# Cross attention and a spline FFN over four batches: a rolled loop with one batch in advance, against an unrolled program that works on three batches at once

## The chip, the cores and the metric

One core of a Trainium2 chip runs the whole kernel. The metric is the device time of one execution in microseconds (us). The kernel before takes 311.19 us (median of 3 runs, 310.43 to 312.0). TensorE (PE) multiplies matrices, VectorE (DVE), ScalarE (ACT) and GpSimd (POOL) work elementwise, and SyncE (SP) starts the DMAs. Each runs its own list of instructions in order; semaphores tie the lists together.

## The reference

For each of 4 batches (512 tokens, width 512) the kernel computes

```
query = ctx @ Wq.T + bq ;  key = ctx @ Wk.T + bk             # ctx 512x256, width 128
att   = softmax(query @ key.T)                               # 512x512
x     = x + einsum('ln,mn->lm', layernorm(x), att)           # no scale, over tokens
gate  = layernorm(x) @ gate_w.T ; up = layernorm(x) @ up_w.T # 2048 wide
x     = x + (silu(gate) * up) @ down_w.T
```

The three FFN weights are Catmull-Rom splines of some 8,000 control points each. The kernel never builds them whole: a weight is a few smooth functions plus a short "residual", so that a projection is a small product with the functions (`project`, `replicate`) and the gate and up products have only 128 rows.

## The kernel before, in words

All sums run in fp32; where a factor is rounded to the 1-pass format (fp32r), a high and a low part are kept, so that many steps are a pair: ACT copies the rounded part out of PSUM, DVE subtracts it from the exact value (`split_prob`, `project`, `half_split`, `down_split`).

- **One list for all engines.** A program calls stages in an order written out by hand (`attention_only`, then `ffn`); every engine has a class with the same stage names and issues only its own part. So the call order is each engine's instruction order.
- **Prologue** (`attention_only`, L429 on): builds the weight tables (`spread`/`residual` 0 to 23, `node_weights`, `jump_inputs`/`jumps`, `down_nodes`), and runs the attention of batch 0. `keep_warm` calls put 60 products of ones on PE between the stages.
- **Pass** (`ffn`, L536 on): the FFN of batch b, and in its gaps the attention of a = b+1. It runs as a hardware loop for b = 0 to 2, then once more for b = 3 without attention.
- In a pass: `project`, `qk` (query and key), four `replicate` (two products, an ACT copy and two DVE operations each, which put the 4 functions of a class into the tile `mv`), 16 gates (`gate_up` on PE, SiLU on ACT, product on DVE: `activate`, L1018; rounding into `ih` on POOL: `round_inter`, L1188), between them `energy`, `softmax`, `prob_t`, `split_prob`; then `down` (64 products with `ih`), `xm` (48 products: attention times x), `add_xm` (adds to x, statistics, `normalise`), `norm_t`/`cast_t` (transposes of the normalised x), `down_tail` (adds the result to `xres` and stores it).
- `prob` is scaled by 1/sum on DVE (`scale`), the low part of x comes from POOL (`low_x`, L1120), and POOL copies x to `xres` in `project` (L1175) once the stores of the batch before are done. POOL also computes the two small reciprocal roots of the layernorms (`ve`, then `rstd`: L1076/L1078 and L1159/L1161).

## Time and profile before

| what | us |
|---|---|
| median of the runs | 311.19 |
| the profiled execution's own time | 310.87 |
| its span, first to last instruction | 308.7 |
| PE busy (82%) | 254.3 |
| DVE busy (65%) | 202.2 |
| POOL busy (50%) | 154.3 |
| ACT busy (45%) | 138.5 |

The span is what the instructions cover; 2.2 us of the execution's time lie around it. Busy time of PE counts pipelined products whose ends are modelled, so it overstates the work. The chain of work that ended last gives PE 36%, POOL 22%, DVE 10%, and 25% to "issue", where the profile shows nothing that was waited for. The granted TensorE clock is 0.912 on average.

### The profile page before, as it was taken

What the parts mean: (1) busy time and instruction counts of PE and PEld (TensorE: products, weight loads), DVE (VectorE), ACT (ScalarE), POOL (GpSimd) and SP (SyncE); (2) the same over time, 40 slices, a digit from 0 to 9 for tenths busy, and PEclk for the clock granted to TensorE, in tenths of its full rate; (3) what the DMA queues carried; (4) which work ended last, traced back from release to release, by engine and by line L of the source; (5) the groups of instructions that cost most, each with busy time, mean ns of one, the idle gap of its engine ahead of it and who ended that gap; (6) DMA issues with size and microseconds to landing.
All of it is one profiled execution on the core that took longest, in us unless ns stands there. A gap on an engine that the chain in (4) does not pass through costs nothing.

```text
span 308.7 us, 4074 instructions
## 1 busy us (share of the span) xinstructions
PE 254.3 (82%) x1320; PEld 158.4 (51%) x1320; DVE 202.2 (65%) x348; ACT 138.5 (45%) x229; POOL 154.3 (50%) x158
## 2 busy tenths in 40 slices
PE   5979519868797889998867999979679999576995
PEld 1323107632333646786334568863436689253484
DVE  1665795674759886575598765756988557478523
ACT  3043414310736586225758642267589131745420
POOL 0987930263675559321463692304829722077810
PEclk9775857995969799999999899999999999959999
DMA  6799600000007000001280000013500000300003
GB/s 221 289 271 381 264 0 0 1 1 2 0 13 328 0 3 0 2 0 68 74 333 0 0 0 0 0 70 95 243 0 0 0 0 14 122 0 2 0 2 136
DMA packets 6938, 22.65 MB, mean 73 GB/s; under 512 B 1168, under 2 KB 2320, under 8 KB 5456
## 3 DMA queue, kind: packets, MB, share of 16 engines
q1 hardware_dynamic: 6928, 22.52, 20.1%
q8 instruction: 6, 0.10, 0.1%
q14 instruction: 4, 0.03, 0.0%
HBM read 18.32 MB, written 4.19 MB: 73 GB/s over the span
## 4 chain that ended last, share of the span: by engine, by line
PE 36%; issue 25%; POOL 22%; DVE 10%; ACT 4%; DMA 1%; SPq 1%; POOLq 0%; DVEq 0%; ACTq 0%
POOL ih L1188 10%; PE bank L1348 5%; POOL xl L1120 4%; PE bank L1350 4%; PE bank L1349 4%; PE bank L1440 4%; POOL xres L1175 3%; PE bank L1222 3%; PE bank L1400 3%; PE bank L1235 2%; POOL gw L1102 2%; PE bank L1325 2%; PE bank L1248 2%; PE bank L1447 1%; PE bank L1414 1%
## 5 line engine op out<-in xcount | busy, mean ns | idle before, releaser
L1188 POOL TENSOR_TENSOR ih<-inter,ones 128x512 fp32r<-128x512 f32 x64 | 64.5, 1040 | 38.4 <-DVE inter L1018 38.4
L1400 PE MATMUL bank<-mv,gw 128*128 128x512 f32 x128 | 47.5, 469 | 17.8 <-DVE inter L1018 9.2
L1018 DVE TENSOR_TENSOR inter<-inter,bank 128x512 f32<-128x512 f32 x64 | 42.1, 682 | 6.6 <-ACT inter L828 5.1
L828 ACT ACTIVATE inter<-bank 128x512 f32<-128x512 f32 x64 | 37.0, 597 | 20.1 <-PE bank L1400 18.6
L1400 PEld LDWEIGHTS bank<-mv,gw 128*128 128x128 f32 x128 | 23.7, 202 | 40.8 <-DVE inter L1018 18.0
L1440 PEld LDWEIGHTS bank<-d_r,ih 128*128 128x128 f32 x256 | 35.3, 188 | 7.9 <-issue 5.0
L1440 PE MATMUL bank<-d_r,ih 128*128 128x288 f32 x256 | 38.2, 299 | 0.0
L799 ACT ACTIVATE qk<-bank,nmr,rstd 128x512 f32<-128x512 f32 x16 | 12.5, 780 | 43.2 <-PE bank L1350 26.9
L1159 POOL TENSOR_TENSOR ve<-mv,eps 128x1 f32<-128x1 f32 x16 | 5.6, 347 | 47.5 <-DVE mv L989 47.5
L1175 POOL TENSOR_TENSOR xres<-x,ones 128x2048 f32<-128x2048 f32 x4 | 14.4, 3600 | 28.8 <-DMA out<-xres 28.5
L1348 PE MATMUL bank<-ph,xh 128*128 128x512 f32 x64 | 25.5, 399 | 2.1 <-POOL xl L1120 2.1
L1010 DVE SCALAR_TENSOR_TENSOR mv<-zd,masks,bank 64x512 fp32r<-64x512 f32 x32 | 23.9, 747 | 4.8 <-ACT zd L821 3.9
L1350 PE MATMUL bank<-ph,xl 128*128 128x512 f32 x64 | 25.0, 391 | 0.0
L1349 PE MATMUL bank<-pl,xh 128*128 128x512 f32 x64 | 24.9, 390 | 0.0
L804 ACT ACTIVATE prob<-bank 128x512 f32<-128x512 f32 x16 | 9.6, 597 | 28.8 <-PE bank L1363 28.6
L1222 PE MATMUL bank<-warm 128*128 128x512 bf16 x60 | 21.0, 515 | 1.5 <-DVE warm L863 1.5
L1235 PE MATMUL bank<-ctxT,wqk 128*128 128x512 f32 x32 | 20.3, 767 | 0.0
L984 DVE TENSOR_TENSOR x<-x,qk 128x512 f32<-128x512 f32 x16 | 11.3, 706 | 12.4 <-ACT qk L799 12.4
L1290 PE MATMUL bank<-knots,spread 64*128 64x288 bf16 x32 | 7.1, 331 | 14.5 <-DVE knots L974 8.7
L1414 PE MATMUL bank<-inter,d_u 64*32 64x512 f32 x256 | 17.6, 635 | 1.2 <-DVE mv L1010 1.2
L1120 POOL TENSOR_TENSOR xl<-xT,xh 128x2048 fp32r<-128x2048 f32 x4 | 18.3, 4570 | 0.0
L1107 POOL TENSOR_TENSOR d_r<-prod 128x288 fp32r<-128x288 f32 x16 | 13.3, 851 | 8.0 <-DVE prod L926 7.7
(98 smaller groups left out, 434.0 us busy)
## 6 DMA issues: line engine op xcount, KB each, us to landing
x<-in_x SPq DMA_DIRECT2D x4, 1024.0 KB, 4.9
xT<-in_xT SPq DMA_DIRECT2D x4, 1024.0 KB, 7.2
out<-xres SPq DMA_DIRECT2D x16, 256.0 KB, 2.0
rd<-in_d_r SPq DMA_DIRECT2D x1, 2304.0 KB, 22.4
ctxT<-in_ctxT SPq DMA_DIRECT2D x4, 512.0 KB, 7.1
d_coef<-in_d_coef SPq DMA_DIRECT2D x1, 1024.0 KB, 15.8
d_pt<-in_d_node SPq DMA_DIRECT2D x1, 1024.0 KB, 17.4
knots<-in_d_knot SPq DMA_DIRECT2D x1, 640.0 KB, 13.2
```

Source lines behind the costliest of these rows:

```text
L828: nc.scalar.activation(inter[:, m], gbank[m % 2][:], ACT.Silu).then_inc(s["silu_done"], 1)
L1010: V.scalar_tensor_tensor(mv[part, 2 * t + n], zs[part, t % 2].bitcast(f32), z_low[part], zbank[t % 2][part], ALU.mult, ALU.add).then_inc(s ...
L1018: V.tensor_tensor(inter[:, m], inter[:, m], ubank[m % 2][:], ALU.mult).then_inc(s["mult_done"], 1)
L1120: G.tensor_tensor(xl[:], xT[:], xh[:].bitcast(f32), ALU.subtract).then_inc(s["xsplit_done"], 1)
L1188: G.tensor_tensor(ih[:, m], inter[:, m], ones[:, 0].broadcast_to([P, TOK]), ALU.mult).then_inc(s["ih_done"], 1)
L1222: mm(zdbank[:], warm[:, 0:P], warm[:], start=True, stop=True)
L1235: last = mm(abank[n][:], wqk[:, n, c], ctxT[:, c], start=c == 0, stop=c == CTX // P - 1)
L1348: mm(abank[t % 2][:], xh[:, n, c], ph[:, n], start=n == 0, stop=False)
L1349: mm(abank[t % 2][:], xh[:, n, c], pl[:, n], start=False, stop=False)
L1350: last = mm(abank[t % 2][:], xl[:, n, c], ph[:, n], start=False, stop=n == NT - 1)
L1400: mm(dst[m % 2][:], gw[:, n, m // 2, m % 2 * P:(m % 2 + 1) * P], mv[:, m // 2], start=True, stop=True).then_inc(s[done], 1)
L1440: mm(in_blocks(obank[t], m % PHASES), ih[:, m, t * P:(t + 1) * P], d_r[:, m], start=m == 0, stop=False, skip_group_check=True)
```

## The change

The loop is unrolled in Python, and the program becomes `attention_first`, then for every b the stages `gates(b)` and `downs(b)`, with a = b+1 and c = b+2:

- `attention_first` runs the attention of batch 0, `project(0)`, and `qk`, `energy`, `softmax` of batch 1. The fillers shrink from 60 to 6; `down_nodes` now stands after the first half of `xm(0)`, and half of the 16 small sums in `residual` moves from POOL to DVE (`upper`).
- `gates(b)` holds the 16 gates of b and, between them, `prob_t`, `xm` and `add_xm` of a. `downs(b)` holds the products of `down` for b, `norm_t`, `cast_t`, `project` and `functions` of a, and `qk`, `energy`, `softmax` of c.
- `replicate` goes. `functions` forms the functions for four classes at a time (4 products, 2 ACT copies, 2 DVE subtractions a batch), and 24 DMAs a batch, of 20 rows of 2 KB, copy them from `zs` to their rows in `mv` (`place` on SP). A gate waits for 12 of them.
- `prob` of batches 1 to 3 is scaled on POOL. x has three buffers, the result is added into x in place, and the `xres` copy goes. `inter` shrinks from 16 to 8 tiles.
- Rounding: POOL rounds every activation of the first three passes; in the last, ACT rounds every fourth.

```diff
-        def attention_only(st):
+        def attention_first(st):
...
+            for n in range(NT):
+                st.xm(0, n, 0)
+            st.jumps()
+            for r in range(8, 10):
+                st.spread(r)
+                st.residual(r)
+            st.turn()
+            st.down_nodes()
+            for t in range(2):
+                st.scale_xm(0, t)
...
+            for t in range(NT):
+                st.energy(1, t)
+                st.softmax(1, t)
+            st.scale(1)
+            st.stats(1)
+            st.mean_shift(1)
+            st.silu_table(0)
...
+        def downs(st, b):
+            a, c = b + 1, b + 2
+            if c < B:
+                st.qk(c, 0)
+            if a < B:
+                st.normalise(a, 3)
+            st.down_basis(b, 3)
+            if c < B:
+                st.qk(c, 1)
+            st.half_split(b)
+            if c < B:
+                st.exp_table()
+            st.down(b, 0)
...
+            if c < B:
+                for t in range(2, NT):
+                    st.energy(c, t)
+                    st.softmax(c, t)
+                st.scale(c)
+                for h in range(2):
+                    st.split_x(c, h)
+            st.down_tail(b, 2)
+            st.add_out(b, 2)
+            st.down(b, 3)
+            if c < B:
+                st.stats(c)
+                st.mean_shift(c)
+                st.silu_table(c)
+            st.down_tail(b, 3)
+            st.add_out(b, 3)
...
+            def place(b, j):
+                sp.wait_ge(s["zs_done"], 2 * b + j + 1)
+                for i in range(CLS):
+                    a = CLS * j + i
+                    base = 0 if a % 2 else HALF
+                    for k, z in enumerate((0, 1, 0)):
+                        rows_to = slice(base + k * G_FN, base + (k + 1) * G_FN)
+                        sp.dma_start(mv[rows_to, a].bitcast(f32), zs[QUAD * i:QUAD * i + G_FN, 2 * j + z].bitcast(f32)).then_inc(s[("z0_in", "z1_in")[j]], 16)
...
                 def scale(b):
-                    pass
+                    if b:
+                        pool.wait_ge(s["rinv_done"], b + 1)
+                        for t in range(NT):
+                            G.tensor_tensor(prob[:, t], prob[:, t], rinv[:, t].broadcast_to([P, TOK]), ALU.mult).then_inc(s["prob_done"], 1)
...
                     for n, (dst, read, done) in enumerate(((gbank, "silu_done", "g_mm"), (ubank, "mult_done", "u_mm"))):
                         if m >= 2:
                             pe.wait_ge(s[read], MT * b + m - 1)
-                        if n == 1 and a is not None:
-                            pe.wait_ge(s["exp_done"], NT * (a + 1))
+                        elif b:
+                            pe.wait_ge(s["out_added"], NT * (b - 1) + 2 * n + m + 1)
```

How the lists of the engines differ is seen at three places. First POOL, in a loop pass of the kernel before, from the last roundings on: `xl` is the low part of x of the next batch, and `ve` and `rstd` (128x4) its layernorm's root.

```order
L1188 TENSOR_TENSOR ih<-inter,ones 128x512 [waits mult_done]
L1119 REGISTER_ALU
L1120 TENSOR_TENSOR xl<-xT,xh 128x2048 [waits xh_done]
L1076 TENSOR_TENSOR ve<-mv,eps 128x4 [waits mv1_done,consts_set]
L1078 TENSOR_TENSOR rstd<-ve,neghalf 128x4 [waits ve1_done]
```

The same place in the changed kernel, after the roundings of pass 0 and up to those of pass 1:

```order
L1270 TENSOR_TENSOR ih<-inter,ones 128x512 [waits mult_done] x2
L1242 TENSOR_TENSOR ve<-mv,eps 128x1 [waits mv2_done]
L1244 TENSOR_TENSOR rstd<-ve,neghalf 128x1 [waits ve2_done]
L1175 TENSOR_TENSOR prob<-prob,rinv 128x512 [waits rinv_done]
L1175 TENSOR_TENSOR prob<-prob,rinv 128x512 x3
L1202 TENSOR_TENSOR xl<-xT,xh 128x1024 [waits xh_done] x2
L1152 TENSOR_TENSOR ve<-mv,eps 128x4 [waits xm_scaled,mv1_done,consts_set]
L1154 TENSOR_TENSOR rstd<-ve,neghalf 128x4 [waits ve1_done]
L1270 TENSOR_TENSOR ih<-inter,ones 128x512 [waits mult_done] x9
```

Four scalings of `prob`, which wait for the sums of all exponentials, now stand ahead of `xl` and of the root, and all of them ahead of the next pass's roundings.

Second DVE at the end of a pass of the kernel before: the results of the batch are added, the last casts done, and the next pass begins with `zp` (`project`).

```order
L1045 TENSOR_TENSOR xres<-xres,bank 128x512 [waits x1_kept,out_mm] x2
L997 CAST mv<-prob 64x512 [waits xn2t_first] x3
L1045 TENSOR_TENSOR xres<-xres,bank 128x512 [waits x1_kept,out_mm] x2
L997 CAST mv<-prob 64x512 [waits xn2t_first]
L638 REGISTER_ALU
L638 COMPARE_AND_BRANCH
L1004 TENSOR_TENSOR zp<-bank,zp 128x512 [waits zp_hi]
```

In the changed kernel, from the first results of pass 0 (`x<-x,bank`) to the first gate products of pass 1 (`inter`):

```order
L1123 TENSOR_TENSOR x<-x,bank 128x512 [waits out_mm] x2
L970 TENSOR_REDUCE nmax<-bank 128x1 [waits energy_mm] x2
L1086 TENSOR_TENSOR zs<-bank,zs 128x512 [waits zs_hi] x2
L970 TENSOR_REDUCE nmax<-bank 128x1 [waits energy_mm] x2
L974 RECIPROCAL rinv<-rsum 128x4 [waits exp_done]
L1123 TENSOR_TENSOR x<-x,bank 128x512 [waits out_mm]
L947 BN_STATS bst<-x 128x6 [waits x2_in]
L947 BN_STATS bst<-x 128x6 x3
L952 BN_AGGR mv<-bst 128x2 [waits stats1,consts_set]
L952 BN_AGGR mv<-bst 128x2 x3
L957 SCALAR_TENSOR_TENSOR nmr<-mv,rstd 128x4 [waits rstd1_done]
L1123 TENSOR_TENSOR x<-x,bank 128x512 [waits out_mm]
```

`nmr`, which waits for POOL's root, now stands ahead of the last addition of the batch; in the kernel before it stood after `half_split` and ahead of the first `add_xm`.

Third SP in a pass of the kernel before, from the load of the next x to the first store:

```order
L684 ISA [waits x1_kept,xn2_done]
L684 DMA x<-in_x 128x2048
L686 DMA xT<-in_xT 128x2048 [waits xn2T_mm]
L688 ISA
L689 ISA [waits qk_mm]
L689 DMA ctxT<-in_ctxT 128x1024
```

and in pass 0 of the changed kernel:

```order
L672 DMA x<-in_x 128x2048 [waits dv_done,res_done]
L708 DMA ctxT<-in_ctxT 128x1024 [waits qk_mm]
L704 DMA xT<-in_xT 128x2048 [waits xsplit_done]
L722 DMA out<-x 128x512 [waits out_added] x2
L718 DMA mv<-zs 20x512 [waits zs_done]
L718 DMA mv<-zs 20x512 x11
L718 DMA mv<-zs 20x512 [waits zs_done]
L718 DMA mv<-zs 20x512 x11
```

The 24 copies of `place` stand behind two stores and ahead of the other two.

## Rows read from the trace of the kernel before

**Rows 1.** Busy time by stretch, us from the span's start.

```profile
core 0: us, PE busy (x) PEld busy (x) DVE busy (x) ACT busy (x) POOL busy (x), PEclk, DMA share, GB/s
0.00:46.00 46.00, 30.03 (x115) 10.28 (x115) 28.00 (x45) 12.87 (x21) 30.41 (x33) 0.74 0.70 239
46.00:93.50 47.50, 40.69 (x159) 22.18 (x159) 29.84 (x48) 15.62 (x25) 20.49 (x25) 0.82 0.03 8
...
118.00:154.00 36.00, 33.12 (x189) 23.75 (x189) 20.91 (x42) 15.51 (x23) 14.48 (x14) 1.00 0.08 30
154.00:178.80 24.80, 20.01 (x107) 11.89 (x106) 20.90 (x36) 17.88 (x33) 14.69 (x15) 0.93 0.27 106
...
273.00:291.70 18.70, 15.90 (x76) 9.23 (x77) 14.95 (x22) 10.29 (x18) 13.65 (x15) 0.85 0.00 1
291.70:308.70 17.00, 13.83 (x106) 10.78 (x105) 4.74 (x7) 1.68 (x3) 2.62 (x3) 1.00 0.17 63
```

**Rows 2.** Timeline of DVE: start, duration; the last gate products of two passes.

```profile
177.49 1.28 DVE L1018 TENSOR_TENSOR inter<-inter,bank 128x512 f32<-128x512 f32 x2
...
287.52 4.17 DVE L1018 TENSOR_TENSOR inter<-inter,bank 128x512 f32<-128x512 f32 x6 [1.90 <-ACT inter L828]
```

**Rows 3.** Costliest groups by line: busy us, mean ns, idle before and its releaser.

```profile
L1188 POOL TENSOR_TENSOR ih<-inter,ones 128x512 fp32r<-128x512 f32 x64 | 64.5, 1040 | 38.4 <-DVE inter L1018 38.4
L1018 DVE TENSOR_TENSOR inter<-inter,bank 128x512 f32<-128x512 f32 x64 | 42.1, 682 | 6.6 <-ACT inter L828 5.1
L1120 POOL TENSOR_TENSOR xl<-xT,xh 128x2048 fp32r<-128x2048 f32 x4 | 18.3, 4570 | 0.0
...
L1078 POOL TENSOR_TENSOR rstd<-ve,neghalf 128x4 f32<-128x4 f32 x4 | 4.1, 1018 | 0.3
```

**Rows 4.** Timeline of PE: query products at both clocks, `xm` products one after another.

```profile
55.19 0.39 PE L1349 MATMUL bank<-pl,xh 128*128 128x512 f32 x1
55.42 0.39 PE L1350 MATMUL bank<-ph,xl 128*128 128x512 f32 x1
...
86.54 3.78 PE L1235 MATMUL bank<-ctxT,wqk 128*128 128x512 f32 x4
...
148.40 1.98 PE L1235 MATMUL bank<-ctxT,wqk 128*128 128x512 f32 x4
```

**Rows 5.** Timeline of ACT: a table load, an exponential, two casts.

```profile
103.81 1.28 ACT L735 ACT_TABLE_LOAD   x1
...
106.67 0.68 ACT L735 ACTIVATE prob<-bank,nmax 128x512 f32<-128x512 f32 x1
...
143.04 0.59 ACT L805 ACTIVATE mv<-bank 64x512 fp32r<-64x512 f32 x1
143.66 0.60 ACT L804 ACTIVATE prob<-bank 128x512 f32<-128x512 f32 x1
```

**Rows 6.** Timeline of POOL and DVE where both read tiles in SBUF.

```profile
35.87 5.36 POOL L1135 TENSOR_TENSOR d_coef<-d_coef,d_pt 128x512 f32<-128x512 f32 x4
36.05 4.06 DVE L966 SCALAR_TENSOR_TENSOR win<-win 64x512 f32<-64x512 f32 x1
...
41.87 0.68 DVE L971 SCALAR_TENSOR_TENSOR win<-knots 64x512 f32<-64x512 f32 x1
...
61.58 2.01 POOL L1107 TENSOR_TENSOR d_r<-prod 128x288 fp32r<-128x288 f32 x2
62.08 0.84 DVE L984 TENSOR_TENSOR x<-x,qk 128x512 f32<-128x512 f32 x1
```

**Rows 7.** Timeline of SP's issues: start, duration.

```profile
8.83 1.75 SPq L647 DMA_DIRECT2D knots<-in_d_knot  x1
...
153.30 0.36 SPq L684 DMA_DIRECT2D x<-in_x  x1
153.75 0.38 SPq L686 DMA_DIRECT2D xT<-in_xT  x1
```

**Rows 8.** DMA issues: KB each, median us from issue to landing.

```profile
out<-xres SPq DMA_DIRECT2D x16, 256.0 KB, 2.0
```

More of the change, by code:

```diff
@@ L528, in attention_only @@
+            st.project(0)
+            for n in range(2):
+                st.qk(1, n)
+            for j in range(2):
+                st.functions(0, j)
+            for h in range(2):
+                st.split_x(1, h)
             for r in range(20, 24):
                 st.spread(r)
[L531 to L540 removed]
+                st.residual(r)
@@ new lines, in gates @@
+            gate(7)
+            if more:
+                st.xm(a, 3, 0)
+                for t in range(2):
+                    st.scale_xm(a, t)
+            gate(8)
+            if more:
+                st.add_xm(a, 0)
+                st.xm(a, 0, 1)
+            gate(9)
+            if more:
+                st.normalise(a, 0)
+                st.add_xm(a, 1)
+                st.xm(a, 1, 1)
+            gate(10)
+            st.down_basis(b, 1)
+            gate(11)
+            if more:
+                st.normalise(a, 1)
+                st.xm(a, 2, 1)
@@ L693, in _ @@
-            sp.wait_ge(s["qk_mm"], 2)
-            sp.dma_start(ctxT[:], d["ctxT"][1]).then_inc(s["ctx_in"], 16)
-            with sp.Fori(0, B - 2) as b:
-                batch(b, True)
-            batch(B - 2, False)
-            for t in range(NT):
-                store(B - 1, t)
-            sp.wait_ge(s["out_stored"], 16 * NT * B + 1)
+                sp.dma_start(out[b, t], x[b][:, t]).then_inc(s["out_stored"], 16)
+            columns(1)
+            sp.wait_ge(s["consts_set"], 1)
+            for j in range(2):
+                place(0, j)
@@ L702, in _ @@
+            for b in range(B):
+                if b + 2 < B:
+                    rows(b + 2)
+                    context(b + 2)
+                    columns(b + 2)
+                for t in range(2):
+                    store(b, t)
+                if b + 1 < B:
+                    for j in range(2):
+                        place(b + 1, j)
+                for t in range(2, NT):
+                    store(b, t)
+            sp.wait_ge(s["out_stored"], 16 * NT * B)
         @block.scalar
```

855 lines of the change are left out of this document (436 added, 419 removed).

## The prediction

> **What bounds the kernel now.** I read the stretches first, then DVE's timeline to cut them at the right points, then the groups by line. The cuts are the ends of a pass's sixteenth gate product on DVE: 118.0 for pass 0 (a border of [rows 1]), 178.8 for pass 1 (177.49 + 1.28) and 291.7 for pass 3 (287.52 + 4.17) [rows 2]. So the kernel is a prologue with the gates of batch 0 (118.0 us), passes of 60.8 us, and 17.0 us from the last product to the end. In the pass from 118.0 to 178.8 PE is busy 33.1 + 20.0 = 53.1 of 60.8 us, DVE 41.8, ACT 33.4, POOL 29.2 [rows 1]. No engine fills it; PE is nearest, at a granted clock of 1.00 and 0.93, nearly the upper level (2.4 GHz). In the prologue the clock is 0.74 and 0.82, a mixture of both levels. POOL waits for DVE's products before its roundings (38.4 us in all), not DVE for POOL [rows 3]. What the deeper pipeline can win is therefore the difference between 60.8 and some 53 a pass, and the prologue's and the last pass's waits. Whether it does hangs on the waits that its order brings, so I followed the changed lists from one cut to the next.
>
> **Between two passes (from product 16 of b to the low part of `prob` of c).** Where PE needs a semaphore only from work that is done, it goes on at 0.23 us for a product of 512 columns (55.19 to 55.42) [rows 4].
> - PE does a quarter of `down_basis` (1.0) and the key half of `qk` (1.8 at the upper level: four parts recorded as 1.98) [rows 4]; ACT then adds the bias (0.7), copies two halves (1.2), loads the exponential's table (1.3 and a small operation, 1.5) and casts 4 x 2 x 0.62 = 5.0 [rows 5]; one more copy (0.6) and one subtraction (0.7) give `zd`: 12.9 us after the cut.
> - Then DVE runs in order: PE's tail and `zp` (1.5), two additions, two maxima, two subtractions of `functions`, two maxima, each pair 1.3 (0.68 for one, 0.60 from one to the next) [rows 2, 3], with ACT's two exponentials (0.68 each [rows 5]) and two copies in between (2), and the last exponential (0.9): 22.0 us.
> - POOL now has `prob`: four operations of the form of `ih`, 4.1 us, then `xl` 4.6, then the root 1.3 [rows 3]: 10 us after the reciprocal. `nmr` on DVE waits for this root. Behind it on DVE stand the last addition of b, which frees the PSUM bank of the second gate's up product, the low parts of `prob`, and every gate product of the next pass; PE can do two transposes and three gate products and then stands. This cover did not exist before: POOL's `xl` and root stood where DVE had `half_split` and statistics. Here DVE has 3.5 us of other work for the 10.
> - Sum: 22.0 + 0.2 + 10.0 + 0.8 = 33 us. It is at least 26 if the POOL chain were hidden, at most 36 if the casts and PE's clock come out worse.
>
> The 24 copies by DMA are hidden. SP gets `zs` at about 19.5 us. Two issues of the loop are 0.45 us apart (153.30 to 153.75) [rows 7], a store lands after 2.0 us [rows 8], so the first twelve are down at 19.5 + 5.4 + 2.0 = 27 us and the other twelve at 32 us, needed only at the ninth gate. If the cover at 33 us goes, the first twelve cost up to 5 us less than they take now, so nothing below 27. No row shows a copy inside SBUF: the lower bound is nothing, the upper 1.75 us an issue, the longest in the trace [rows 7], by which they would be down at 42 us. I take 0.45, since the queue is not full there as it was then.
>
> **Gates.** PE has 32 gate products and 48 of `xm`, 80 x 0.23 = 18.2 us, transposes and partial products of some 5: 23.6. DVE has 16 products and 4 low parts, at 0.60 from one to the next 12, and three of the four additions to x with their statistics and normalisations, some 2.2 each: 18.5. They don't lie side by side. DVE works behind PE until the first half of `xm` is done, some 16 us in; after that the additions and normalisations hold back gate products (in order on DVE), and the rest is DVE's own 11 to 12 us with a wait for a root here and there. So 16.5 + 12 + 1 for a port that it shares with POOL (below) = 29.5. The lower bound is 24.8, what the gates with four maxima, four low parts and their exponentials take now [rows 1]; the upper 33. What `replicate` gave back (six DVE operations net, 4 us a pass, and an ACT copy or two) is in this sum. POOL's 16 roundings take 16.6 us [rows 3] and are no bound; the four that ACT takes over in the last pass save nothing there. The `xres` copy ended before POOL had a product to round [rows 3], so its going counts as nothing.
>
> So a pass takes 33 + 29.5 = 62.5 us, against 60.8.
>
> **Prologue, up to the low parts of `prob` of batch 1.** Milestones: 14 us, both `qk` products of batch 0, now ahead of all tables and at the lower clock level (3.78 us for four parts [rows 4] instead of 1.98); 34, the tables, softmax and node weights, a chain of DVE operations; 43, the root, four jump inputs on POOL, low parts of `prob`; 49, the first half of `xm`; then a new wait. POOL does two sums and the four multiplications of `down_nodes` (5.4 us [rows 6]), DVE and ACT, in order, wait for them and do 3.9 more, and only then may ACT scale `xm` and free the banks: 60.5, with PE idle for 11 us and back at the lower level. 68, the second half of `xm`; 78, additions, roots and residuals in turn; 84, casts; 94, `project`, `qk`, `functions`; 108, softmax of batch 1, held by the last residuals, whose POOL half stands behind `xl`; 112 to 113, `prob` on POOL and the root. I take 112; the bounds are 100 (the upper clock level throughout, and half of the new wait gone) and 120. The gates of batch 0 end at 112 + 29.5 = 141.5 us, 23.5 later than now, but with `xm` of batch 1 done.
>
> **The end.** Pass 3 has no attention. After product 16 of pass 2 the chain to `zs` is short by the exponentials and the query (14 us), the first twelve copies take 5.4 + 2.0: 21.5. The gates of batch 3: 0.7 each for 16, 1.4 for the first to pass through, 1 for the lower clock after PE's wait of 3 us: 13.5. Then 17.0 as now [rows 1].
>
> **Sum.** 112 + 29.5 + 2 x 62.5 + 21.5 + 13.5 + 17.0 = 318.5 us of span, against 308.7. With the 2.2 us around the span of the profiled execution (310.87) it is 320.7; that execution stands 0.3 below the median of 311.19, which leaves the forecast at 320.
>
> **What speaks against the change beside this.** In the trace a DVE operation on two tiles in SBUF that began 0.18 us after POOL's four multiplications took 4.06 us, where the next of its kind took 0.68; an addition to x under two POOL sums took 0.84 [rows 6]; gate products, with one input in PSUM, keep 682 ns beside the roundings [rows 3]. The Trainium skill's page "SBUF — State Buffer", section "Who interferes with whom", says that a DVE instruction with two SBUF inputs, or a `tensor_scalar` in a 2-port mode, and a GpSimd instruction that reads SBUF exclude each other for the whole instruction. The trace agrees in the first case and hardly in the second (0.16 us).
>
> **Rivals.**
> - A: the pipeline does what its depth allows. For it speaks that no engine has over 53.1 us in a pass [rows 1]; against it the root behind `xl`. If the POOL chain is covered, 27 + 27 us a pass: 112 + 27 + 2 x 54 + 52 = 299, so 301 us.
> - B (slower still): additions and normalisations now run while POOL rounds without pause. If each of the seven of a pass waits for half to a whole rounding of 1.04 us, or now and then loses to several as at 36.05 [rows 3, 6], it is 3 to 4 us more a pass in three passes, less the 1 counted: 328 us. It decides as soon as DVE, not PE, sets the second half of the gates.
> - C: the prologue keeps pace, at 102 instead of 112: 310 us, no change.
> - D: the small copies are slow, 1.75 us an issue [rows 7]: 42 instead of 33 us twice, and 14 us later in the last pass: 353 us. The skill's page "DMA: Bandwidth & Descriptors", section "Rules for kernel authors", says that transfers under 64 KB pay mostly overhead and are to be merged; these have 40 KB. No row here shows one.
>
> **How the numbers follow.** The forecast has 0.48 (its own range 313 to 327), A 0.20, B 0.20, C 0.09, D 0.03. From the low bound of A to above B, 301 to 335 us, leaves out some 2 in 10. A measurement of this kernel can tell 0.5% from no change, 309.6 to 312.7 us. Faster: A, and a third of C: 0.23. Same: the rest of C and the forecast's edge: 0.08. Slower: 0.69.
>
> **What would show it.** Right: `nmr` in passes 1 and 2 waits some 6 us for POOL's root and PE stands meanwhile after the third gate product; products 16 lie 61 to 64 us apart; ACT's first scaling of `xm` in the prologue follows POOL's `d_coef`; the first gate stands near 112. Wrong: gates that follow each other without this wait, passes of 54 us, or a first gate before 100.

## The result and the profile after

The changed kernel takes 330.75 us (median of 4, 329.06 to 331.17) against 310.81 of the kernel before on the same chip: 1.064 times as long, 95% interval 1.058 to 1.069. The sign and the range held; the size did not: 19.9 us were lost where the forecast had 8.8. The profiled execution took 329.06 us, its span 327.3 us; it was the fastest of the four (the others' spans are 328.6 to 329.4 us), so what follows takes apart some 1.7 us less than the median lost.

The span of after in stretches. The cuts are the forecast's own: the first low part of `prob` (115.1), the end of the sixteenth gate product of a pass on DVE (143.5, 204.2, 265.3, 310.5), the low parts again (176.0, 236.7, two rows left out), the first gate of the last pass (292.7; PE started it at 292.56). Columns as in [rows 1].

```profile
0.00:46.00 46.00, 26.61 (x108) 12.84 (x109) 32.95 (x62) 14.23 (x25) 20.32 (x22) 0.70 0.80 282
46.00:115.10 69.10, 38.76 (x132) 22.29 (x131) 36.33 (x62) 19.66 (x34) 32.00 (x36) 0.70 0.07 15
115.10:143.50 28.40, 26.36 (x141) 17.50 (x140) 20.60 (x33) 14.32 (x24) 18.49 (x21) 0.95 0.25 91
143.50:176.00 32.50, 25.91 (x151) 19.59 (x151) 16.97 (x36) 18.69 (x33) 11.99 (x11) 0.89 0.14 38
176.00:204.20 28.20, 26.03 (x137) 17.11 (x137) 20.40 (x34) 12.64 (x21) 18.45 (x21) 0.94 0.34 123
...
265.30:292.70 27.40, 20.81 (x125) 16.14 (x126) 10.12 (x18) 8.14 (x14) 2.16 (x3) 0.87 0.13 39
292.70:310.50 17.80, 15.54 (x80) 7.12 (x80) 10.72 (x16) 10.58 (x19) 12.18 (x12) 0.83 0.19 56
310.50:327.30 16.80, 13.54 (x96) 11.63 (x96) 4.74 (x8) 2.31 (x4) 0.04 (x1) 0.96 0.16 63
```

Set beside the forecast, term by term (us of span; the last column sums to the 8.8 that are missing between 318.5 and 327.3):

| term | forecast | measured | difference |
|---|---|---|---|
| prologue to the low parts of batch 1 | 112 | 115.1 | +3.1 |
| gates of batch 0 | 29.5 | 28.4 | -1.1 |
| between passes, gates (pass 1) | 33 + 29.5 | 32.45 + 28.25 | -1.8 |
| between passes, gates (pass 2) | 33 + 29.5 | 32.45 + 28.6 | -1.45 |
| last pass: to its first gate | 21.5 | 27.3 | +5.8 |
| last pass: its 16 gates | 13.5 | 17.95 | +4.45 |
| the end | 17.0 | 16.8 | -0.2 |

So 13.35 us were missing in three terms, and 4.55 us that the others had too much hid a third of it: the total is nearer to the forecast than its terms are.

Pass 1 is as long as before, 60.7 us against 60.8, and pass 2 is 1.8 us longer; PE has 25.9 + 26.0 busy us in pass 1, one less than the 53.1 of [rows 1]. What the change gives in the last pass (53.7 before, 45.2 now) does not pay for a prologue that is 25.5 us longer (118.0 to 143.5). The unrolling does not show as a cost of its own: "issue", where nothing that the profile shows was waited for, has 5% of the chain that ended last, against 25% before. The groups by line and the waits (columns of the waits: us in total, times, longest), to be read against [rows 3]:

```profile
L1270 POOL TENSOR_TENSOR ih<-inter,ones 128x512 fp32r<-128x512 f32 x60 | 65.6, 1108 | 55.5 <-DVE inter L1094 55.2
...
L1094 DVE TENSOR_TENSOR inter<-inter,bank 128x512 f32<-128x512 f32 x64 | 42.7, 681 | 27.4 <-ACT inter L881 26.7
...
DVE nmr L957 <- POOL rstd L1154: 17.2, 4, 6.6
...
PE bank L1442 <- ACT qk L849: 10.4, 1, 10.4
...
PE bank L1510 <- DMA mv<-zs: 9.2, 4, 5.9
```

Three waits stand there that the kernel before did not have at this size: DVE for POOL's root, PE in the middle of `xm` of the prologue, and PE for the small copies. The first was there before, but short:

```profile
DVE nmr L895 <- POOL rstd L1078: 4.4, 3, 1.5
```

The first two were forecast, each within 0.6 us. The third was forecast to be hidden.

The timeline between pass 0 and pass 1, POOL, then DVE, then PE:

```profile
165.36 4.03 POOL L1175 TENSOR_TENSOR prob<-prob,rinv 128x512 f32<-128x512 f32 x4 [19.38 <-DVE rinv L974]
169.35 4.67 POOL L1202 TENSOR_TENSOR xl<-xT,xh 128x1024 fp32r<-128x1024 f32 x2
173.98 0.20 POOL L1152 TENSOR_TENSOR ve<-mv,eps 128x4 f32<-128x4 f32 x1
174.25 1.01 POOL L1154 TENSOR_TENSOR rstd<-ve,neghalf 128x4 f32<-128x4 f32 x1
...
175.30 0.16 DVE L957 SCALAR_TENSOR_TENSOR nmr<-mv,rstd 128x4 f32<-128x4 f32 x1 [6.59 <-POOL rstd L1154]
...
172.58 1.62 PE L1510 MATMUL bank<-mv,gw 128*128 128x512 f32 x3 [1.17 <-DMA mv<-zs]
176.12 0.80 PE L1510 MATMUL bank<-mv,gw 128*128 128x512 f32 x1 [1.91 <-DVE x L1123]
```

This is the forecast's chain: four scalings, `xl`, the root, then `nmr` after 6.59 us, and PE stops after the third gate product, since the addition that frees the fourth's bank stands behind `nmr` on DVE. PE's first product there already waited 1.17 us for the copies; the wait for the root came behind that and ended last.

The last pass: SP's 24 issues, with those of the prologue ahead for comparison; PE's first 16 partial products and 16 products of `down`, with 16 later ones of `down`; then PE's first gates and its ninth.

```profile
95.48 18.16 SPq L718 DMA_DIRECT2D mv<-zs  x24
...
281.94 17.97 SPq L718 DMA_DIRECT2D mv<-zs  x24
...
265.33 1.96 PE L1530 MATMUL bank<-inter,d_u 64*32 64x512 f32 x16 [3.34 <-DVE inter L1094]
267.23 4.21 PE L1560 MATMUL bank<-d_r,ih 128*128 128x288 f32 x16
...
280.86 2.28 PE L1560 MATMUL bank<-d_r,ih 128*128 128x288 f32 x16
...
292.56 6.39 PE L1510 MATMUL bank<-mv,gw 128*128 128x512 f32 x14 [5.91 <-DMA mv<-zs]
...
301.35 1.69 PE L1510 MATMUL bank<-mv,gw 128*128 128x512 f32 x5 [0.71 <-DMA mv<-zs]
```

The issues stand 0.75 us apart (17.97 / 24; 0.76 in the prologue, where SP's issue before them ended 57 us earlier), not the 0.45 that the forecast took from two loads [rows 7], so the first twelve are down 10.6 us after the first issue instead of 7.4. That is 3.2 of the 5.8 us. The other 2.6 are a chain to `zs` of 16.7 us (265.3 to 281.9) where the forecast had 14, and the trace shows where they arose. After 3.34 us of waiting PE is granted 0.50, the lower level (1.2 GHz), from 265.3 to 271.3: the 16 partial products take 1.96 us instead of the 1.09 of the other passes, and 16 products of `down` 4.21 instead of 2.28. That is 2.8 us, and the transposes of the normalised x stand behind them. In the prologue run below, which changes nothing in the last pass, the same 16 products of `down` took 2.88 us, and the chain 15.3.

### The profile page after: what moved, and what is told of

It reads as the page before. It is cut to its first block, busy times and chain, and to the rows that moved or that the text cites. A ratio compares the mean times of both kernels' runs of the same rounds, so it can differ in the third digit from the quotient of the medians.

```text
span 327.3 us, 3646 instructions
## 1 busy us (share of the span) xinstructions
PE 243.9 (75%) x1250; PEld 160.2 (49%) x1250; DVE 190.3 (58%) x328; ACT 131.2 (40%) x226; POOL 146.1 (45%) x158
## 4 chain that ended last, share of the span: by engine, by line
PE 45%; DVE 21%; POOL 11%; ACT 10%; SPq 6%; issue 5%; DMA 2%; DVEq 0%; ACTq 0%; POOLq 0%
PE bank L1560 7%; PE bank L1510 6%; SPq L718 5%; PE bank L1320 4%; POOL xl L1202 4%; PE bank L1442 4%; PE bank L1443 3%; PE bank L1444 3%; PE bank L1530 3%; DVE inter L1094 3%; DVE bst L947 3%; PE bank L1398 2%; PE bank L1566 2%; DVE bst L1060 2%; PE bank L1346 2%
## 5 line engine op out<-in xcount | busy, mean ns | idle before, releaser
L881 ACT ACTIVATE inter<-bank 128x512 f32<-128x512 f32 x64 | 37.2, 596 | 45.3 <-PE bank L1510 44.9
L1442 PE MATMUL bank<-ph,xh 128*128 128x512 f32 x64 | 27.5, 430 | 10.4 <-ACT qk L849 10.4
L1175 POOL TENSOR_TENSOR prob<-prob,rinv 128x512 f32<-128x512 f32 x12 | 12.1, 1041 | 44.1 <-DVE rinv L974 44.1
L1398 PE MATMUL bank<-masks,prob 128*128 128x128 f32 x64 | 14.5, 391 | 19.1 <-POOL prob L1175 10.7
L1202 POOL TENSOR_TENSOR xl<-xT,xh 128x1024 fp32r<-128x1024 f32 x8 | 18.7, 2357 | 13.5 <-ACT xh L809 13.5
L1398 PEld LDWEIGHTS bank<-masks,prob 128*128 128x128 f32 x64 | 11.4, 203 | 23.3 <-POOL prob L1175 12.3
L781 ACT ACTIVATE prob<-bank,nmax 128x512 f32<-128x512 f32 x16 | 10.9, 686 | 25.6 <-DVE nmax L970 25.6
L801 ACT ACTIVATE ph<-bank 128x512 fp32r<-128x512 f32 x16 | 9.6, 598 | 28.4 <-PE bank L1398 28.4
L1320 PE MATMUL bank<-ctxT,wqk 128*128 128x512 f32 x32 | 18.1, 705 | 3.6 <-DMA wqk<-in_wkT 3.6
L1442 PEld LDWEIGHTS bank<-ph,xh 128*128 128x128 f32 x64 | 13.4, 209 | 14.3 <-ACT qk L849 10.7
L997 DVE TENSOR_TENSOR prod<-bank,rd 128x576 f32<-128x576 f32 x16 | 11.7, 750 | 11.6 <-PE bank L1384 7.1
L1466 PE MATMUL bank<-masks,xn 128*128 128x128 f32 x64 | 11.4, 316 | 8.9 <-DVE xn L1071 6.0
```

What stands on the lines that cost most here:

```text
L881: nc.scalar.activation(inter[:, m % DEPTH], gbank[m % 2], ACT.Silu).then_inc(s["silu_done"], 1)
L1202: G.tensor_tensor(xl[:, part], xT[:, part], xh[:, part].bitcast(f32), ALU.subtract).then_inc(s["xsplit_done"], 1)
L1320: last = mm(abank[n], wqk[:, n, c], ctxT[:, c], start=c == 0, stop=c == CTX // P - 1)
L1398: last = nc.tensor.transpose(pbank[t % 2][:, m * P:(m + 1) * P], prob[:, m, t * P:(t + 1) * P], ident)
L1442: mm(abank[t % 2], xh[:, n, c], ph[:, n], start=n == 0, stop=False)
```

## The experiments

All kernels are the changed one with the edit shown. The edits are shortened: `...` stands for lines left out, and within lines types, semaphores and helper code are left out too. The gates of batch 0 ended between 143.4 and 145.7 us in the profiled runs of after and of seven kernels that change nothing ahead of them on the engines, and the medians come from several chips, on which the kernel before took 309.4 to 311.7 us; so the runs are compared by their stretches: gates of batch 0 done, then from one sixteenth product to the next, then to the end.

| kernel | median us | span | gates of 0 done | pass 1 | pass 2 | last pass | end |
|---|---|---|---|---|---|---|---|
| before | 310.81 | 308.7 | 118.0 | 60.8 | 59.3 | 53.7 | 17.0 |
| after | 330.75 | 327.3 | 143.5 | 60.7 | 61.05 | 45.2 | 16.8 |
| early root | 322.92 | 320.7 | 143.4 | 57.8 | 57.9 | 44.8 | 16.7 |
| two queues | 328.40 | 326.9 | 144.7 | 60.7 | 61.0 | 43.7 | 16.7 |
| early taps | 327.16 | 324.8 | 140.6 | 60.9 | 61.2 | 45.3 | 16.8 |
| 16 copies | 324.93 | 323.2 | 143.5 | 60.7 | 61.05 | 41.2 | 16.7 |
| no ACT rounding | 330.46 | 329.4 | 145.7 | 60.7 | 61.1 | 45.2 | 16.8 |
| gates ahead | 327.50 | 325.5 | 145.05 | 60.7 | 61.1 | 42.0 | 16.7 |
| prologue | 317.05 | 315.7 | 132.8 | 61.1 | 61.2 | 43.8 | 16.8 |
| first four together | 303.56 | 302.6 | 134.2 | 55.55 | 54.85 | 41.3 | 16.8 |
| scale on DVE | 334.59 | 332.7 | 146.4 | 62.3 | 61.9 | 45.3 | 16.8 |
| copies hidden | 324.00 | 323.1 | 145.7 | 60.7 | 61.0 | 38.9 | 16.8 |
| four banks | 325.10 | 323.7 | 145.0 | 60.7 | 61.0 | 40.2 | 16.8 |
| all, scale on DVE | 304.70 | 301.9 | 131.8 | 58.5 | 58.3 | 36.5 | 16.8 |
| all, scale on POOL | 296.99 | 293.3 | 131.3 | 54.8 | 54.9 | 35.6 | 16.7 |
| all, `xl` behind | 297.83 | 295.4 | 134.6 | 54.0 | 54.4 | 35.6 | 16.8 |

**Early root.**

```diff
             st.half_split(b)
             if c < B:
+                st.stats(c)
                 st.exp_table()
...
             st.down_split(b)
+            if c < B:
+                st.mean_shift(c)
             st.down(b, 1)
...
             if c < B:
-                st.stats(c)
-                st.mean_shift(c)
                 st.silu_table(c)
```

> The layernorm statistics of batch c and their root on GpSimd are moved ahead of the scaling of prob and of xl (to the casts of the same pass, where GpSimd has nothing to do for 19 us); nothing else changes. Theory (the forecast's step between two passes): nmr no longer waits 6.6 us for the root, so the low parts of prob start when ACT has copied the first half, near 171.2 instead of 175.98, and the third addition no longer holds PE; the first gate stays where it is, since it waits for the copies (172.6). Passes 1 and 2 get some 3 us shorter each (57.5 and 58 instead of 60.7 and 61.05 between the sixteenth products), 6.5 us in all: span 321, time 324. Rival: the gates behind it are bound by PE (26.4 of 28.4 us busy), or xm waits for xl instead, and most of it is given back: under 2 us in all, 329.

Measured: 2.9 and 3.1 us off the two passes, 6.6 of span. DVE and PE at the same place:

```profile
155.81 0.15 DVE L958 SCALAR_TENSOR_TENSOR nmr<-mv,rstd 128x4 f32<-128x4 f32 x1
...
171.13 0.69 DVE L1008 TENSOR_TENSOR pl<-bank,ph 128x512 fp32r<-128x512 f32 x1 [3.47 <-ACT ph L802]
...
172.48 2.04 PE L1511 MATMUL bank<-mv,gw 128*128 128x512 f32 x4 [1.16 <-DMA mv<-zs]
```

`nmr` waits for nothing, the low parts start at 171.13 instead of 175.98, and PE's first gate has not moved, since it waits for the copies. The step stands as forecast: the root's place alone cost 3 us a pass. The low parts came 4.85 us earlier; the other 2 were kept by the copies, as the four edits together show below.

**Two queues for the copies of the last pass.**

```diff
-                for i in range(CLS):
+                copies(sp, b, j, range(2 if b in SHARED else CLS))    # SHARED = (3,)
...
+                    if t == 2 and b + 1 in SHARED:                    # act, down_tail
+                        for j in range(2):
+                            act.wait_ge(s["zs_done"], 2 * (b + 1) + j + 1)
+                            copies(act, b + 1, j, range(2, CLS))
```

> Of the 24 copies of the last pass 12 (classes 2 and 3 of each four) are issued by ScalarE, which is idle there, and 12 by SyncE; passes before are unchanged. Theory (the copies are late because one queue issues them 0.75 us apart): six issues and the landing take 4.5 + 1.6 us, so the first gate of the last pass starts near 288 instead of 292.6, the ninth gate waits for nothing, and the sixteenth product comes 6 us earlier: span 321, time 324.5. Rival (the DMA engines or SBUF take that long for 20 rows of 2 KB, or both queues share one issuer): the copies land as late as before, and nothing changes within 1.5 us.

```profile
283.19 10.05 ACTq L661 DMA_DIRECT2D mv<-zs  x12
293.37 1.09 ACT L886 ACTIVATE inter<-bank 128x512 f32<-128x512 f32 x2 [10.45 <-issue]
...
290.47 2.05 PE L1518 MATMUL bank<-mv,gw 128*128 128x512 f32 x4 [2.61 <-DMA mv<-zs]
```

The copies did land earlier: PE's first product came 7.3 us after the first issue instead of 10.6. But ScalarE issued all its twelve, for both halves, in 10.05 us before the first SiLU, which starts at 293.37, the same time as in after (this pass began 1.2 us later). Of the 6 us 1.5 were seen (45.2 to 43.7). The edit exchanged one wait for another; it shows that the queue's issues were late, not what hiding them is worth.

**Early taps.** POOL's four multiplications get a stage of their own behind `jump_inputs`; `down_nodes` (sums on DVE, copy on ACT) moves behind the residuals 12 and 13.

```diff
             st.jump_inputs()
+            st.down_taps()            # POOL: the four multiplications
...
-            st.down_nodes()
             for t in range(2):
                 st.scale_xm(0, t)
...
+            st.down_nodes()
```

> In the prologue the four multiplications on GpSimd stand right behind the jump inputs (where GpSimd was idle for 6.8 us), and the sums on VectorE and the copy on ScalarE behind the second half of xm; nothing else changes. Theory (the wait of 10.4 us of PE in the middle of xm sets the prologue): ScalarE scales the first half near 51 instead of 60.6, and everything up to the first gate comes 9 to 10 us earlier: first low part of prob near 106, span 318, time 321. Rival (another chain sets the prologue: the 16 residuals on VectorE and GpSimd, or the multiplications now hold VectorE's jump operations as long as before): under 3 us.

ScalarE scaled at 53.16 instead of 60.63, yet the first low part came at 111.8 instead of 115.1. Of the 7.5 us 3.8 went to the sums and their wait for ScalarE, which now stand between two additions to x, and 1 to query products at the lower clock level. And not all of the expected 9 to 10 arose in the first place, because POOL now runs beside DVE's jump operation:

```profile
45.49 4.11 DVE L1039 SCALAR_TENSOR_TENSOR win<-win 64x512 f32<-64x512 f32 x1
...
45.28 5.47 POOL L1220 TENSOR_TENSOR d_coef<-d_coef,xn 128x512 f32<-128x512 f32 x4
```

That is the pair of [rows 6] once more: 4.11 us for an operation that takes 0.68 alone. The rival's bound, under 3 us, is nearer than the theory's; with the run-to-run difference of the prologue the size is not settled by this run.

**16 copies instead of 24.**

```diff
-                    for k, z in enumerate((0, 1, 0)):
-                        rows_to = slice(base + k * G_FN, base + (k + 1) * G_FN)
-                        sp.dma_start(mv[rows_to, a], zs[QUAD * i:QUAD * i + G_FN, 2 * j + z])
+                    part = slice(QUAD * i, QUAD * i + G_FN)
+                    sp.dma_start(mv[base:base + 2 * G_FN, a], zs[part, 2 * j:2 * j + 2])
+                    sp.dma_start(mv[base + 2 * G_FN:base + 3 * G_FN, a], zs[part, 2 * j])
```

> 16 copies a batch instead of 24: the high and low functions of a class go in one DMA of 40 rows (the rows of the table are reordered to match), the second high part in one of 20 rows; the bytes are the same. If an issue costs 0.75 us whatever it carries, a batch takes 12 us instead of 18, the first gate of the last pass starts 3 us earlier (289.6) and the ninth waits for nothing: 4 to 5 us in the last pass and 1 us in each of the two before, span 321 to 322. If the rows set the cost, the 40-row copies take 1.4 us, a batch still 18, and the time does not change within 1 us.

An issue of 40 rows, one of 20 rows, and the first gate of the last pass:

```profile
165.14 0.79 SPq L718 DMA_DIRECT2D mv<-zs  x1
165.97 0.72 SPq L719 DMA_DIRECT2D mv<-zs  x1
...
289.91 1.66 PE L1511 MATMUL bank<-mv,gw 128*128 128x512 f32 x5 [3.27 <-DMA mv<-zs]
```

Twice the rows cost 0.07 us more, so between 20 and 40 rows it is the number of issues that counts. The last pass is 4.0 us shorter and the ninth gate waits for nothing; the passes before do not change, since there the root's wait ends last. The 1 us expected in each of them was wrong for that reason.

**No rounding on ScalarE.**

```diff
         def on_scalar(b, m):
-            return m % 4 == 3 if b == B - 1 else False
+            return False
```

> GpSimd rounds all activations of the last pass too (ScalarE none); nothing else changes. Theory (as forecast, that the four which ScalarE takes save nothing): GpSimd needs 16 x 1.04 us beside gates that take 16.5 us from the first to the last product, so the time stays within 1 us of the changed kernel, 330. Rival 1: the four copies of 0.63 us hold ScalarE's SiLU and make part of the 3 us that the gates of the last pass are longer than forecast: 2 to 3 us less. Rival 2: GpSimd falls behind and the last rounded tile comes late: 2 to 4 us more.

The last pass takes 45.2 us with and without. Who rounds there moves nothing, as forecast.

**Gate products ahead** (on top of the 16 copies): in the last pass PE issues the gate product of m+1 before the up product of m.

```diff
-                    one(0, m)                                            # gate product
+                    for g in range(m + 1 if m else 0, min(m + 2, MT)):   # last pass
+                        one(0, g)
                     one(1, m)                                            # up product
```

> The 16 copies, and in the last pass alone PE issues the gate product of m+1 ahead of the up product of m, so that SiLU of m+1 no longer waits for the product of VectorE with m-1. Compared with the kernel of 16 copies alone (span 323.2), where the 16 gates of the last pass take 16.5 us from the first PE product to VectorE's last. Theory: two PSUM banks for each of gate and up make a ring PE 0.49, ScalarE 0.60, VectorE 0.69 us with some 0.2 between, 2 us for two gates; with the gate products ahead VectorE is the bound (0.69 to 0.75 a gate), and the gates take 13 us: span 320, time 321.5. Rival: GpSimd's roundings with 8 buffers, or the partial products of down_basis that stand between the gates on PE, set the pace: less than 1 us gained.

A miss: from PE's first product to DVE's last 17.4 us instead of 16.55. The trace shows ScalarE waiting 0.43 to 0.62 us for DVE ahead of each of its copies, and PE up to 0.65 us for the SiLU behind them, with the up product now behind that.

**Prologue.** As "early taps", but `down_nodes` behind `project(0)`, and

```diff
-            for h in range(2):
-                st.split_x(1, h)
             for r in range(20, 24):
                 st.spread(r)
                 st.residual(r)
+            for h in range(2):
+                st.split_x(1, h)
```

> Prologue alone: the four multiplications of GpSimd right behind the jump inputs, as before, but the sums on VectorE and the copy on ScalarE behind project (where VectorE waited 3 us) instead of in the middle of the additions to x; and xl of batch 1 on GpSimd behind the last four residuals instead of ahead of them (VectorE waited 4.2 us for them). Theory: the 7.5 us that the early multiplications gained at the scaling of xm (53.2 instead of 60.6) were eaten to 3.4 by these sums and by the query products at the lower clock; now 3 to 4 us of that come back, and the order of xl gives 3.4: first low part of prob near 105 instead of 115.1, span 317, time 320. Rival: the softmax of batch 1 is held by PE's energies and ScalarE at the lower clock anyway: span 321, time 323.

The low parts start at 103.6, the gates of batch 0 end 10.7 us earlier than in after, and the time falls to 317.05 us. So 11 of the 115 us were order alone: the wait in `xm`, the sums in the wrong place, and `xl` ahead of the last residuals.

**The first four together** (early root, 16 copies, prologue, gates ahead).

> The early root, the 16 copies, the reordered prologue and the gate products ahead in the last pass, all together. If each takes away a wait of its own, the gains add up: 6.6 + 4.1 + 10 + 3.5, and 1 to 2 us more in each of passes 1 and 2, where the first gate then waits neither for the root nor for the copies: span near 300, time 303, 2.5% faster than the kernel before. Rival: the waits overlap (PE falls to the lower clock or the next wait takes their place) and half of it comes: span 313, time 315, still slower than the kernel before.

303.56 us, 0.984 times the kernel before (0.973 to 0.994). The gains add up, though gate products ahead alone had made the last pass 0.8 us longer: passes of 55.55 and 54.85 us, since the first gate now waits for neither root nor copies.

**Scale on DVE** (one part of the change undone).

```diff
                 def scale(b):                       # vector; on gpsimd: pass
-                    if b == 0:
+                    if True:
```

> One part of the change undone: prob of batches 1 to 3 is scaled on VectorE (four operations of 0.42 us, as in the prologue) instead of GpSimd (four in 4.03 us). Theory: xl on GpSimd then waits for nothing but ScalarE's copy (166 us in pass 0) and the root is done near 172.2 instead of 175.3, the scaled prob 2.3 us earlier; 3 us less in each of passes 1 and 2 and 2.3 in the prologue: span 319, time 322. Rival: the 1.7 us more on VectorE stand in front of its additions and low parts, and PE's transposes follow prob anyway: under 3 us in all, 328.

The opposite: 1.6 and 0.9 us more a pass. DVE's four scalings beside POOL's `xl`:

```profile
168.20 5.91 DVE L978 TENSOR_SCALAR prob<-prob,rinv 128x512 f32<-128x512 f32 x4
...
168.98 4.84 POOL L1199 TENSOR_TENSOR xl<-xT,xh 128x1024 fp32r<-128x1024 f32 x2 [20.13 <-ACT xh L809]
```

5.91 us instead of 1.68, longer than the 4.03 on POOL, and the statistics, `nmr` and low parts behind them. One of the four executions of this kernel took 1156 us; it has no trace, and its cause is open. The others took 332.2 to 334.7.

**Copies hidden.** The 16 copies, and in the last pass ScalarE issues four of the first eight, once.

```diff
-                for i in range(CLS):
...
+                copies(sp, j, range(2 if b == B - 1 and j == 0 else CLS))
...
+                    if t == 2 and b + 1 == B - 1:        # act, in down_tail
+                        act.wait_ge(s["zs_done"], 2 * (b + 1) + 1)
+                        copies(act, 0, range(2, CLS))
```

> 16 copies a batch, and in the last pass four of the first eight are issued by ScalarE (idle there until the first SiLU), the rest by SyncE. Compared with 16 copies alone (span 323.2; the first gate of the last pass started 3.9 us later than PE had its last product done, at 289.9). Theory (the issues alone make the copies late): four issues of 0.8 us and the landing of 1.5 to 2.3 us, so the first gate starts near 287.5, when the additions of batch 2 free the banks anyway: span 320.5, time 322.5; the term of copies in the last pass is then gone. Rival: the landing grows with two queues at once (2.3 us where one queue showed 1.5) and under 1 us is gained.

The last pass takes 38.9 us, 2.3 less than with 16 copies alone; PE still waits 1.65 us. The first gate now starts 23.1 us into the pass (267.4 to 290.5). The median fell by 0.9 us only, and in the profiled run the gates of batch 0 ended 2.2 us later. A second thing changed with it. Mean granted clock over the gates of the last pass, in after, with 16 copies, and here (columns as above):

```profile
292.50:295.50 3.00, 2.94 (x7) 1.97 (x7) 1.34 (x2) 1.62 (x3) 0.73 (x1) 0.50 0.26 61
295.50:299.90 4.40, 4.40 (x25) 1.98 (x23) 3.42 (x6) 2.99 (x6) 3.96 (x5) 0.63 0.23 53
```

```profile
289.90:306.50 16.60, 14.77 (x80) 6.71 (x80) 10.54 (x16) 10.48 (x20) 12.26 (x12) 0.90 0.21 61
```

```profile
290.50:306.40 15.90, 13.97 (x81) 5.74 (x81) 10.37 (x16) 10.48 (x20) 12.21 (x12) 1.00 0.19 56
```

After 5.9 us without work PE runs its first gates at 0.50, the lower level, and then at 0.63; after 1.65 us it stays at the upper (2.4 GHz). The gates' share of the loss is partly the copies' too: 17.95, 16.55, 15.84 us.

**Four up banks** (on top of the 16 copies).

```diff
+        uring = bank[2:4] + bank[6:8]
...
+            return uring[m % 4] if b == B - 1 else ubank[m % 2]
...
+                        deep = 4 if n and b == B - 1 else 2
+                        if m >= deep:
+                            pe.wait_ge(s[read], MT * b + m + 1 - deep)
```

> 16 copies, and in the last pass the up products go round four PSUM banks instead of two, so PE may be four up products ahead of VectorE. Compared with 16 copies alone, where the 16 gates of the last pass take 16.5 us from PE's first product to VectorE's last, 0.86 us from one product to the next while they follow each other. Theory (the forecast's 13.5 us for these gates failed by the ring of two banks, PE to ScalarE to VectorE to PE, and by the partial products of 1.09 us that stand between): with four banks VectorE is the bound at 0.6 to 0.7 us a gate, the gates take 13 us, span 320, time 321.5. Rival: the gate banks, still two, or the partial products in PE's order hold it: under 1 us.

1.05 us (16.55 to 15.5), not 3.5. For its first 14 products PE is the bound, at the lower level: 5.96 us, 0.43 each, 0.85 a gate. With 16 copies alone, after nearly the same wait (3.27 us), the first five products still ran at the upper level, and the mean clock over the gates was 0.90 against 0.82 here; so this run shows less than the banks are worth.

```profile
291.43 5.96 PE L1518 MATMUL bank<-mv,gw 128*128 128x512 f32 x14 [3.33 <-DMA mv<-zs]
```

**All, scale on DVE** (early root, prologue, copies hidden, four banks, scale on DVE).

> All that helped: early root, reordered prologue, 16 copies with four of them on ScalarE in the last pass, prob scaled on VectorE throughout, four up banks in the last pass, PE's order of the gates as in the changed kernel. From the 302.6 us of span with the first four parts (its last gates 16.7 us): 2.4 us less in the prologue and in each of two passes by the scaling, 2.4 by the copies, 3 by the banks: span 290, time 292, 6% faster than the kernel before. Rival: once the scaling is short, xl (4.7 us) on GpSimd or the lower clock of PE takes over and half comes: 297.

304.70 us: the theory fell. The last pass and the prologue gained as expected, but each pass lost 3 us against the four together, by the scaling beside `xl`.

**All, scale on POOL** (the same without the scaling).

> All that helped, prob of batches 1 to 3 scaled on GpSimd as in the changed kernel: early root, reordered prologue, 16 copies with four of them on ScalarE in the last pass, four up banks in the last pass. If the terms add up: gates of batch 0 end near 134, two passes of 55.5 and 54.9 as with the first four parts, 36.5 to the last product as with the copies and banks, 16.8 to the end: span 298, time 299.5. Rival: the passes depend on what was left out, and it is no better than 302.

296.99 us, 0.955 times the kernel before (0.949 to 0.962), the fastest kernel of this study. The last pass takes 35.6 us: 21.8 to the first gate, and 13.8 for the gates with four banks and PE at the upper level throughout them:

```profile
241.00:262.80 21.80, 19.37 (x124) 14.70 (x125) 10.14 (x19) 8.13 (x14) 2.15 (x3) 0.92 0.17 53
262.80:276.60 13.80, 12.67 (x80) 5.53 (x80) 10.18 (x16) 10.35 (x19) 11.50 (x12) 1.00 0.22 64
```

The forecast had 21.5 and 13.5. So the forecast's two terms fit this kernel, where PE waits 1.75 us for the copies, and not the changed one; in part that is luck. The chain to `zs` took 15.4 us (forecast 14) and the copies 6.4 (forecast 7.4), and the 13.8 have four banks and no lower level, where the forecast had two banks and 1 us for the clock. Against "copies hidden" (15.84 us, also at 1.00) the four banks are worth 2.0 us.

**All, `xl` behind the scaling.** Scale on DVE, and for batches 2 and 3

```diff
                 def split_x(b, h):                      # gpsimd
+                    if b > 1:
+                        pool.wait_ge(s["prob_done"], NT * (b + 1))
```

> As the run beside it, but prob is scaled on VectorE throughout, and for batches 2 and 3 xl on GpSimd waits until the scaling is done. Theory (VectorE's scaling and GpSimd's xl exclude each other at SBUF; that alone made the undone scaling slower): the four operations take 1.7 us again instead of 5.9, the low parts of prob start 25.4 us after the sixteenth product instead of 27.7, and xl is still done before its product needs it: 2.3 us less than the run beside it in each of two passes and in the prologue, span 291, time 293. Rival (the place in VectorE's order costs, or xl is now what xm waits for): no gain, 298 or more.

```profile
156.38 1.68 DVE L991 TENSOR_SCALAR prob<-prob,rinv 128x512 f32<-128x512 f32 x4
...
158.13 4.70 POOL L1214 TENSOR_TENSOR xl<-xT,xh 128x1024 fp32r<-128x1024 f32 x2 [13.40 <-DVE prob L991]
...
161.03 1.17 PE L1528 MATMUL bank<-mv,gw 128*128 128x512 f32 x4 [1.83 <-DMA mv<-zs]
```

The scaling takes 1.68 us again with its place in DVE's order unchanged: running beside `xl` was the cause. The low parts start 25.45 us after the product instead of 27.2, but PE's first gate waits 1.83 us for the copies, and only 0.8 and 0.4 us of a pass come. The time is that of "all, scale on POOL", since the gates of batch 0 ended 3.3 us later here, with PE at a mean granted clock of 0.54 in their first 7 us; no run took this apart.

## Why the forecast was wrong, by its own steps

- **Between two passes: right.** 32.45 us against 33 (the terms named add to 12.5 us up to `zd`, where 12.9 is written, and 12.5 was measured), `nmr` waits 6.59 and 6.58 us for the root, and PE stands after the third gate product. Moving the root took the wait away and 3 us a pass with it. That the root was covered before holds only nearly: DVE waited up to 1.5 us for it.
- **Gates: right within 1.3 us.** 28.25 to 28.6 against 29.5. The forecast put 1 us on the shared port: three of the four normalisations of a pass take 1.1 to 1.25 us where they run beside a rounding, 0.55 otherwise, which is 1.8 us of DVE, and the additions keep 0.68; how much of it the pass felt, no run separates. Rival B, a port that sets the pass, did not occur.
- **Who rounds: no effect, as forecast.** ScalarE's four roundings in the last pass save nothing.
- **"The 24 copies by DMA are hidden": failed.** The forecast took 0.45 us an issue from two large loads, with the reason that the queue is not full. Measured: 0.75, also where SP had issued nothing for 57 us. Rival D had the mechanism (small copies are slow), at a price of 1.75 that was too high; the truth lay between the bounds that the forecast had named. In passes 1 and 2 the error showed as 1.2 us of PE's wait, with the root's wait behind it. In the last pass nothing covers it.
- **The last pass to its first gate: 27.3, forecast 21.5.** 3.2 by the copies' pitch, and 2.6 in the chain to `zs`, where PE fell to the lower level after a wait of 3.34 us. In this pass the forecast allowed for that level only behind the wait for the copies.
- **Its 16 gates: 17.95, forecast 13.5.** Three causes, each seen: the lower level after the long wait, at which PE and not DVE sets the gate (0.85 us), the wait of the ninth gate for its copies (0.71), and two banks. With the copies shortened and the clock up it was 15.84, and 13.8 with four banks as well. The forecast allowed 1 us for the clock and nothing for the others; its 0.7 us a gate holds for a DVE that hardly waits.
- **Prologue: 115.1 against 112.** The new wait (10.4 us of PE; forecast 11) and its end (60.6; forecast 60.5) came as worked out. The 3 us came behind it. The second half of `xm` was done at 70.1 instead of 68: after the wait its first twelve products stand 0.43 us apart, the last twelve 0.23. The casts ended at 86.8 instead of 84. An open rival is the fillers, part of the change too: PE's mean clock in the prologue is 0.70 in both stretches, where it was 0.74 and 0.82 with 60 of them, and no run put them back.
- **Rival A was possible, but in another order.** Its 54 us a pass, for a POOL chain that is covered, are nearly the 54.8 of the best kernel. The pipeline's depth was sound; the order inside it was not.

The sum: the step that failed is the cover of the copies, with what hung on it. Of the 10.2 us by which the last pass was mis-sized, 6.3 went when the copies alone were shortened and split (45.2 to 38.9), the clock that rose with it included, and 3.3 more with the other edits, the four banks (2.0) among them (to 35.6).

The forecast weighed two pages. The Trainium skill's page "DMA: Bandwidth & Descriptors", section "Rules for kernel authors", says that transfers under 64 KB pay mostly overhead and should be merged, and that spreading DMAs over engines saves only issue time. The traces agree with both: 0.72 us for 20 rows and 0.79 for 40, and two queues shortened the wait by the issues. The Trainium skill's page "SBUF — State Buffer", section "Who interferes with whom", says that a `tensor_scalar` in a 2-port mode and a GpSimd instruction that reads SBUF exclude each other. The scaling of `prob` (1.68 alone, 5.91 beside `xl`) agrees, though no trace shows an operation's port mode. The additions of two SBUF inputs kept 0.68 us; there POOL's rounding was the longer one, 1.42 instead of 1.04.

## What to carry to other kernels

Price a small DMA by its issue, not by its bytes, and by a row of its own kind: a large load's issue (0.34 to 0.43 us) says nothing of that of a 40 KB copy (0.71), and twelve issues in a row are a wait of their own wherever no other work stands in front of them. When a stage is moved to an engine that is "free", look at what stands behind it in that engine's list: here four scalings put `xl` and a root, needed by all of the next pass, 4 us further back, and the remedy was to start the root earlier, not to move the scaling back. Set a deeper pipeline's longer prologue against what the passes and the last pass give: the best kernel has 13.3 us more in the prologue and 6.0, 4.4 and 18.1 less behind it; the changed kernel had 25.5 more, and only the last pass gave something back (8.5).

## What the hardware showed that was not expected

- A copy from SBUF to SBUF of 20 rows of 2 KB holds SP's queue for 0.71 us, a 1 MB load for 0.34 to 0.43, and a load of 0.5 KB in the prologue 0.43 too. So it is not the bytes; whether it is the tile in SBUF as the source or the 20 rows, no run separates. ScalarE started nothing else while it issued: twelve took it 10.05 us.
- Normalising (one SBUF input, two per-partition scalars) beside POOL's rounding took twice its time, and the next one alone did not:

```profile
141.69 1.25 DVE L1071 TENSOR_SCALAR xn<-x,mv,rstd 128x512 f32<-128x512 f32 x1 [0.34 <-POOL rstd L1244]
...
146.01 0.55 DVE L1071 TENSOR_SCALAR xn<-x,mv,rstd 128x512 f32<-128x512 f32 x1 [0.29 <-POOL rstd L1244]
...
141.62 1.04 POOL L1270 TENSOR_TENSOR ih<-inter,ones 128x512 fp32r<-128x512 f32 x1
```
